# A graph network's edge messages: every tile is summed as two parts, and VectorE works on two tiles at a time

## What is computed

```python
def _L3_gnn_ref(node_feats, edge_index, edge_attr, W_edge, b_edge, eps, ...):
    src, dst = (edge_index[0], edge_index[1])
    edge_emb = edge_attr @ W_edge + b_edge          # 40000 x 128 @ 128 x 512
    msg = jax.nn.relu(node_feats[src] + edge_emb)
    aggr = jax.ops.segment_sum(msg, dst, num_segments=N)
    h = (1.0 + eps) * node_feats + aggr
    ...
```

## Time and profile before

| | before |
|---|---|
| median of 3 runs | 2900.51 us (2897.43 to 2900.98) |
| the profiled execution | 2902.25 us, its span 2900.6 us |
| busy of the span | PE 88%, DVE 74%, ACT 57%, POOL 44% |
| stage of the edge messages | 1994.2 to 2543.9 us of the span |
| groups in it | 94, of four tiles each |

### The profile page before, as it was taken

One profiled execution on the slowest core, in us unless ns is written; L12 is line 12 of the kernel. 1 busy time (PEld: TensorE's weight loads), 2 busy tenths in 40 slices (PEclk: granted clock), 3 DMA queues, 4 the chain that ended last, 5 costly groups with the idle time before them and its releaser, 6 DMA issues. The chain is left out here.

```text
span 2900.6 us, 46161 instructions
## 1 busy us (share of the span) xinstructions
PE 2562.1 (88%) x13119; PEld 2006.2 (69%) x13119; DVE 2148.1 (74%) x4185; ACT 1659.2 (57%) x3689; POOL 1286.6 (44%) x1273
## 2 busy tenths in 40 slices
PE   6999899989699999869999988597999999977587
PEld 4588555554588999538899964376888888655476
DVE  9798899978338888443688855756999999765837
ACT  1399888861227777212577750225888888724340
POOL 1777000007207767520477654416777777410101
PEclk9999999999799999979999999798999999978798
DMA  2300000032435443324445455226888888811001
GB/s 87 94 19 7 8 0 0 0 91 80 145 136 144 137 141 116 105 82 172 106 143 138 124 100 70 84 94 210 276 277 275 279 275 275 192 37 48 24 28 50
DMA packets 125597, 338.58 MB, mean 117 GB/s; under 512 B 24071, under 2 KB 38346, under 8 KB 125454
## 3 DMA queue, kind: packets, MB, share of 16 engines
q0 software_dynamic: 60768, 172.88, 21.1%
q1 hardware_dynamic: 64686, 163.93, 17.5%
HBM read 243.04 MB, written 85.82 MB: 113 GB/s over the span
## 5 line engine op out<-in xcount | busy, mean ns | idle before, releaser
L1738 POOL DMA_INDIRECT x_got<-table_dram,src_idx x376 | 417.1, 1109 | 119.5 <-issue 88.0
L760 POOL DMA_INDIRECT feature_rows<-in_edge_attr,ids x376 | 370.9, 986 | 117.3 <-issue 109.7
L1868 DVE TENSOR_TENSOR msg<-bank,x_got 128x512 f32<-128x512 f32 x376 | 252.9, 683 | 70.8 <-PE bank L1763 47.2
L1273 DVE TENSOR_TENSOR pt_low<-bank,pt_high 128x640 fp32r<-128x640 f32 x320 | 248.7, 818 | 66.3 <-ACT pt_high L1237 64.7
L669 ACT ACTIVATE hot_rest<-hot_dst,slot_w 128x128 bf16<-128x128 bf16 x864 | 272.6, 400 | 37.0 <-DVE hot_dst L629 37.0
L763 POOL COPY ids<-id_idx 128x136 uint32 (+2 forms) x5 | 1.2, 242 | 644.8 <-DVE id_idx L856 363.5
L1237 ACT CAST pt_high<-bank 128x640 fp32r<-128x640 f32 x320 | 206.5, 697 | 100.1 <-PE bank L1190 100.1
L1267 DVE CUSTOM_DVE_ANT_0 p<-bank,log_counts 128x1254 f32<-128x1254 f32 x160 | 232.7, 1454 | 23.6 <-PE bank L1174 23.5
L1817 ACT ACTIVATE msg_high<-msg 128x512 fp32r<-128x512 f32 x329 | 206.7, 628 | 72.7 <-DVE msg L1868 72.6
L1848 DVE SCALAR_TENSOR_TENSOR msg_low<-msg,msg_high 128x512 fp32r<-128x512 f32 x329 | 223.5, 680 | 0.0
L1229 ACT ACTIVATE p<-p,bound 128x1254 f32<-128x1254 f32 x160 | 217.0, 1356 | 10.9 <-DVE bound L1267 10.8
(11 more groups left out here) (416 smaller groups left out, 6685.5 us busy)
## 6 DMA issues: line engine op xcount, KB each, us to landing
features_dram<-feature_parts POOLq DMA_DIRECT2D x94, 512.0 KB
edge_got<-features_dram SPq DMA_DIRECT2D x94, 512.0 KB, 5.2
qk_dram<-qk_high SPq DMA_DIRECT2D x16, 640.0 KB, 2.9
qk_dram<-qk_low SPq DMA_DIRECT2D x16, 640.0 KB, 4.2
keys<-qk_dram SPq DMA_DIRECT2D x32, 320.0 KB, 4.9
queries<-qk_dram SPq DMA_DIRECT2D x32, 320.0 KB, 6.8
queries_low<-qk_dram SPq DMA_DIRECT2D x32, 320.0 KB, 8.4
acc_a<-zeros SPq DMA_DIRECT2D x1, 6400.0 KB, 30.0
```

What stands on the lines that cost most here:

```text
L760: pool.indirect_dma_start(out=rows[:, g % 2, j * ED:(j + 1) * ED], out_offset=None, in_=self.a.edge_attr_128, in_offset=bass.IndirectOffse ...
L1273: dve.tensor_tensor(p_low[:, made % 3, :, columns], unit(u).rearrange("p (j n) -> p j n", n=P), p_high[:, made % 3, :, columns].bitcast(F3 ...
L1738: pool.indirect_dma_start(out=xg[:, g % XRING, j, :], out_offset=None, in_=k.table_dram, in_offset=bass.IndirectOffsetOnAxis(ap=k.src_idx[ ...
L1868: dve.tensor_tensor(msg[:, j, :], k.bank[:, 2 + j, :], xg[:, r, j, :], ALU.add).then_inc(added_x, 1)
```

## The change

All tiles are now treated alike, as a high and a low part: `msg_whole` and the float32 matmul are gone. DVE adds two tiles (a pair, banks 2 and 3 or 4 and 5) in one instruction of 1024 elements a partition, and makes the low parts of two tiles in one. `added_x` and `low_done` count pairs now, and PE, ACT and POOL wait for pairs. DVE waits until both tiles of a pair are embedded. ACT still makes the high parts tile by tile. The order in group g on DVE is add pair 0, lower(g - 1, pair 1), sum(g - 2), add pair 1, lower(g, pair 0).

The diff, cut to its core:

```diff
@@ gpsimd @@
                     if g >= XRING:
-                        pool.wait_ge(added_x, 2 * GT + t - XRING * GT + 1)
+                        pool.wait_ge(added_x, PAIRS * (g - XRING + 2) + j // 2 + 1)
@@ tensor, embed @@
                 for j in range(GT):
-                    pe.wait_ge(added_x, g * GT + GT + j + 1)
+                    if j % 2 == 0:
+                        pe.wait_ge(added_x, g * PAIRS + PAIRS + j // 2 + 1)
@@ tensor, collect @@
                 for j in range(GT):
-                    if is_whole(u, j):
-                        pe.wait_ge(relu_done, g * GT + j + 1)
-                        m = pe.matmul(k.bank[:, 6 + u, :], hot[:, u, j, :].bitcast(F32), whole[:], start=(j == 0), stop=(j == GT - 1))
-                    else:
-                        pe.wait_ge(low_done, i * PAIR + lowered(u, j))
-                        pe.matmul(k.bank[:, 6 + u, :], hot[:, u, j, :], high[:, u, j, :], start=(j == 0), stop=False)
-                        m = pe.matmul(k.bank[:, 6 + u, :], hot[:, u, j, :], low[:, u, j, :], start=False, stop=(j == GT - 1))
+                    if j % 2 == 0:
+                        pe.wait_ge(low_done, g * PAIRS + j // 2 + 1)
+                    pe.matmul(k.bank[:, 6 + u, :], hot[:, u, j, :], high[:, u, j, :], start=(j == 0), stop=False)
+                    m = pe.matmul(k.bank[:, 6 + u, :], hot[:, u, j, :], low[:, u, j, :], start=False, stop=(j == GT - 1))
@@ vector @@
+            def lower(g, u, p):
+                two = slice(2 * p, 2 * p + 2)
+                dve.wait_ge(relu_done, g * GT + 2 * p + 2)
+                dve.scalar_tensor_tensor(low[:, u, two, :], msg[:, two, :], 0.0, high[:, u, two, :].bitcast(F32), ALU.max, ALU.subtract).then_inc(low_done, 1)
@@ vector, group @@
+                for p in range(PAIRS):
+                    two = slice(2 * p, 2 * p + 2)
+                    dve.wait_ge(emb_done, g * GT + 2 * p + 2)
+
+                    if not first:
+                        dve.wait_ge(low_done, g * PAIRS - PAIRS + p + 1)
+                    dve.tensor_tensor(msg[:, two, :], k.bank[:, 2 + 2 * p:4 + 2 * p, :], xg[:, r, two, :], ALU.add).then_inc(added_x, 1)
+                    if p == 1:
+                        lower(g, u, 0)
                     elif not first:
-                        lower(g - 1, 1 - u, j + 2)
-                    if j == 1 and sums:
+                        lower(g - 1, 1 - u, 1)
+                    if p == 0 and sums:
                         add_sum(g - 2, u)
```

More of the change, by code:

```diff
@@ L1670, in _ @@
                     norms[2].apply(dve, b, x[:, b, :]).then_inc(x3_ready, 1)
-WHOLE = 0
 XRING = 4
[L1678 to L1687, removed]
 def edge_messages(nc, k, a):
@@ L1815, in relu @@
                 for j in range(GT):
-                    act.wait_ge(added_x, g * GT + 2 * GT + j + 1)
-                    act.activation(whole[:] if is_whole(u, j) else high[:, u, j, :], msg[:, j, :], ACT.Relu).then_inc(relu_done, 1)
+                    act.wait_ge(added_x, g * PAIRS + 2 * PAIRS + j // 2 + 1)
+                    act.activation(high[:, u, j, :], msg[:, j, :], ACT.Relu).then_inc(relu_done, 1)
                     if j == 0:
@@ L1856, in add_sum, with group @@
                 dve.tensor_tensor(rows, k.bank[:, 6 + u, :], rows, ALU.add).then_inc(agg_added, 1)
-            def group(g, u, r, got, pairs, first=False, sums=True):
+            def group(g, u, r, got, first=False, sums=True):
                 dve.wait_ge(got_x[r], got * (16 * GT))
[L1861 to L1865, removed]
-                    elif not first:
[L1867 to L1871, removed]
-                        lower(g - 1, 1 - u, j + 2)
-                    if j == 1 and sums:
+                for p in range(PAIRS):
[6 more added lines that the diff above has]
+                        lower(g, u, 0)
+                    elif not first:
+                        lower(g - 1, 1 - u, 1)
+                    if p == 0 and sums:
                         add_sum(g - 2, u)
             dve.memset(one[:], 1.0).then_inc(one_set, 1)
-            dve.sem_inc(added_x, 2 * GT)
+            dve.sem_inc(added_x, 2 * PAIRS)
             dve.memset(agg, 0.0).then_inc(agg_added, 2)
@@ L1883, in _ @@
             dve.tensor_tensor(w_low[:], we[:], w_high[:].bitcast(F32), ALU.subtract).then_inc(w_split, 1)
-            group(0, 0, 0, 1, 0, first=True, sums=False)
-            group(1, 1, 1, 1, 0, sums=False)
+            group(0, 0, 0, 1, first=True, sums=False)
+            group(1, 1, 1, 1, sums=False)
             with dve.Fori(0, (NG - 2) // XRING) as i:
@@ L1888, in _ @@
                     n = 2 + v
-                    group(i * XRING + n, n % 2, n % XRING, i + n // XRING + 1, i * (XRING // 2) + (n - 1) // 2)
-            lower(NG - 1, 1, GT - 2)
-            lower(NG - 1, 1, GT - 1)
+                    group(i * XRING + n, n % 2, n % XRING, i + n // XRING + 1)
+            lower(NG - 1, 1, 1)
             add_sum(NG - 2, 0)
```

2 lines of the change are left out of this document (1 added, 1 removed).

## The result

| | before | changed |
|---|---|---|
| median of the runs | 2900.02 us (4 runs, 2897.43 to 2900.98) | 2933.11 us (4 runs, 2926.84 to 2933.52) |
| span of the profiled execution | 2900.6 us | 2931.0 us |

The ratio is 1.0107, with a 95% interval of 1.0094 to 1.0120: slower by 33 us. The forecast was 2930.5 with a range of 2918 to 2943.

A forecast was written before the change was run, and what follows sets the result against it. PE was taken to bound the first part at 5.69 us a group, gathers the last nine groups. A PE wait for paired low parts gives 6.05: 0.36 x 80 = 29, plus about 1, so 2930.5 us, range 2918 to 2943.

The forecast's parts named there:

- The bound before: Stage's first part, up to group 84: PE bounds it without gaps, at 5.69 us a group.
- the tail: Last nine groups: slow gathers set the pace, 7.32 us each, and pass the earlier delay on.
- gathers run four groups ahead: POOL's gathers are issued four groups early, so the delay counts for about 80 groups: 29 us.
- The loop: Embed, paired add, low part, PE's release at 4.16 us, four matmuls, turn: PE stands still about 0.44 us a group.
- PE's loop branch: Turn takes 0.94 instead of 0.84 us where PE's loop branches after a wait; half taken every second group.
- The sum: 0.36 us a group over 80 groups, 29 us, plus about 1 for filling and emptying the pipeline.
- The signs: Expected in the changed profile: among others, PE idle 6 to 8% of the first part, DVE gap about 0.9 us.
- stay the bound: Rival: low parts come early enough that PE never waits; 5.45 to 5.47 us a group, 2882 us; 6%.
- DVE's busy time: Rival: DVE's fixed instruction cost decides, so merging saves 0.44 us in two groups, 2883 us; 1%.
- The clock: Rival: PE's idling lowers its clock; one group in ten at the lower level gives 2975 us; 3%.
- cancelled: Rival: PE's saving and stall meet, or the slow last gathers take up the delay; 2896 to 2905 us; 3%.
- A longer period eases POOL: POOL gets some slots about half a microsecond later, but the longer group time relieves it and the DMA engines.

The follow-up runs named there:

- x1: Kernel before with every tile in two parts, no float32 matmul, adds and low parts still one tile at a time: 2887.43 us, ratio 0.9955.
- x2: Changed kernel with adds still paired but low parts made and counted tile by tile: 2902.33 us, ratio 1.0007.
- s: Changed kernel with DVE's sum moved ahead of the low parts PE waits for, run twice on slower chips: 3197.14 and 3197.18 us, ratios 1.0040 and 1.0035.
- x4: Changed kernel with tile 0 of each even group again summed by one float32 matmul: 2929.05 us, ratio 1.0098.
- x3: Changed kernel with adds tile by tile and low parts still paired, the first right behind tile 0's add: 2975.36 us, ratio 1.0245.
- e1: Changed kernel with pair 1's low parts ahead of the next group's first add, run twice on slower chips: 3153.84 and 3152.87 us, ratios 0.9897 and 0.9890.

## Why the prediction was right

- **The bound before and the tail.** That PE bounds the first part was right: with the same unpaired order and 0.44 us less of PE's work in two groups, x1 went down by 0.2 us a group. The tail handed the delay on, 66.00 against 65.87. That gathers run four groups ahead was wrong. In the trace of before a gather is issued some 10 us after its slot is free and ends 10.4 to 11.1 us ahead of its add, under two groups. As 0.34 a group over 82 instead of 80 groups is still 28, the sum didn't suffer.
- **The loop.** 1.75 to the pair's add, measured 1.75; 1.14 for the add, measured 1.13 to 1.14; release at 4.16, measured 4.15; four matmuls 1.03, measured 1.04; turn 0.84, measured 0.84. The pitch of a 1024 instruction was the one term without a row of its own and came out as 0.08 less than its duration.
- **The period.** 6.05 was forecast, 6.03 measured. The term that was mis-sized is the 0.02 for PE's loop branch: no group of the steady part shows it, while x2, with two matmuls between wait and branch, shows 0.10 in every second group.
- **The sum.** From the stage's first add to the end of its last sum it was 551.0 us before and is 580.6 now, 29.6 more, where +30 was forecast. The rest of the 33 us lies outside the change: the medians of four runs spread by more than that (2926.84 to 2933.52), and the profiled spans differ by 30.4.
- **The signs.** Two were forecast too large: PE idle for 6 to 8% of the first part (4.7%) and a DVE gap of 0.9 (0.81). Both are worked out from starts, while the profile subtracts the drawn durations: PE loses 0.43 of 6.03 us, 7%, of which 0.28 is drawn as idle, and DVE's gap from the end of its pitch is 0.81 + 0.08.
- **The cause.** s puts a dose on the path and gets it back one for one in the distance of the groups; x2 takes half of a merged instruction off it and gains 31 us; x4 gives PE its work back and loses nothing. These three show the cause of the 6.03, x2 and x4 in the whole time on chip 0; before them it was only read from the timeline.
- **The rivals.** PE didn't stay the bound: x1 shows what that looks like, and it has no merged instruction. DVE's busy time rose by 3 us: what the pairing saves in two groups (8 x 0.06) nearly pays for the added low part (0.60). And DVE has a gap in every group, so its work sets nothing. The clock stayed at 1.00 with PE idle for 4.7% of the part. Nothing was cancelled on chip 0; on the other chips the whole change came out as no change, which the prediction had at 3% and for another reason.
- **What was too easy.** "A longer period eases POOL" left out that the low parts hold the gathers. It cost nothing in this forecast, but the same reading missed x3 by 93 us. POOL's gathers (402.82 / 337 = 1.20 us, and 0.30 behind each) fill the changed kernel's period too, since two of four are drawn out to 0.82 behind a low part's end. Still POOL doesn't set the pace there: from group 3 to 84 no add waits for a gather, and the 288 gathers of groups 8 to 79 landed at least 3.6 us ahead of their adds. How much less than 6.03 POOL would allow with these merged low parts isn't shown.

The best kernel found on chip 0 is x1: 2887.43 us, 0.45% under before and 1.5% under the changed one. On the other chips it is e1, 1.0 to 1.1% under both. Neither was run where the other was.

## What to carry to other kernels

Merging two instructions saves only what their starts show, not their fixed cost as drawn: here two of 512 take 1.20 us from the first's start to the start of what follows, and one of 1024 takes 1.14. What it surely does is to move two signals to the time of the later one; follow the in-order consumer from its last input to the moment when it wants the first half, and compare. When a change joins a part that removes work with a part that reorders it, time them apart, since the sum hid a gain of 14 us behind a loss of 46.

## What the runs showed of the hardware

- A gather issued by POOL takes 0.95 us. One that begins more than 0.03 us after the start of a DVE low part, which has both operands in SBUF, lasts until about 0.82 after that instruction's end: 1.97 us in x3. One that began before the low part isn't held, and neither is one beside an add or a sum, which read a bank (162 gathers of 0.94 to 0.96 in the changed kernel). Through two low parts back to back it is held only when it begins right behind the first one's start (2.04 us, 15 of 77). Before, with single low parts between adds, the longest was 1.45 us. The prediction had given DVE's order no effect on POOL at all.
- So POOL had only gaps of 0.30 us in before and in the changed kernel, though no add waited for it: the holds took up what slack it had. A full engine alone isn't a bound.
- The kernel before took 2901 us on one chip and 3186 on three others. In the changed kernel the distance between undisturbed groups was the same (6.03). Its span grew by 253 us, 205 of them ahead of the stage and 47 in it. Those lie in the stage's start, where the first two groups take 25 us instead of 10, and the long groups. s and e1 have such a start but no long groups behind it up to group 84. The source is open.
